# A graph network and a mixture of experts on one core: the experts' second layer as three products of halves, split on chip

## What is computed

```python
# x: (16, 512, 128), adj: (16, 512, 512), all float32
x = x + gnn(layernorm(x), adj)      # convolution of 17 taps, exp(-dist) * adj, GRU gates
x = x + ffn(layernorm(x))           # 8 experts, top 2 of them per token
# in ffn, with xn normalized once more, gamma and beta applied, w_full the weights of the two chosen experts:
for e in range(8):
    h = gelu(xn @ W1[e] + b1[e], approximate=False)      # 128 -> 256
    y = y + (h @ W2[e] + b2[e]) * w_full[..., e, None]   # 256 -> 128
```

## Time and profile before

| | us |
|---|---|
| median of the runs | 666.71 |
| lowest and highest | 663.08, 667.06 |
| the profiled execution, its own time | 669.05 |
| its span on the core | 667.3 |

### The profile page before, as it was taken

How to read it: one execution, slowest core, us unless ns; L and a number is a source line. 1 busy time by engine, 2 the same in 40 slices (tenths; PEclk the granted TensorE clock), 3 DMA queues, 4 the chain that set the end, 5 groups by cost and what they waited for, 6 DMA issues and landing times.

```text
span 667.3 us, 13068 instructions
## 1 busy us (share of the span) xinstructions
PE 623.3 (93%) x3784; PEld 530.2 (79%) x3784; DVE 498.2 (75%) x2050; ACT 418.4 (63%) x824; POOL 344.6 (52%) x273
## 2 busy tenths in 40 slices
PE   3799898989999999999999999999999988799996
PEld 2679687777979797979797888888888777688874
DVE  6958888888888888888888888888888755333322
ACT  4544546485858485858485858585767546466663
POOL 3200314145847474748474747574757545556750
PEclk9898999999999999999999999999999979899999
DMA  8327231538379747474755666666555578863341
GB/s 305 115 92 245 82 124 52 179 101 232 75 203 340 195 117 189 122 191 120 182 130 152 154 153 159 156 156 158 149 140 153 147 184 200 224 144 53 52 77 57
DMA packets 105399, 101.04 MB, mean 151 GB/s; under 512 B 8896, under 2 KB 83904, under 8 KB 105024
## 3 DMA queue, kind: packets, MB, share of 16 engines
q1 hardware_dynamic: 82736, 83.28, 40.4%
q0 software_dynamic: 22592, 16.92, 16.7%
HBM read 75.85 MB, written 30.51 MB: 159 GB/s over the span
## 4 chain that ended last, share of the span: by engine, by line
PE 63%; DVE 17%; issue 7%; DMA 5%; POOL 4%; ACT 3%; SPq 0%; another core or an unknown queue 0%; DVEq 0%; ACTq 0%; POOLq 0%
PE Y L598 9%; PE G L708 5%; PE C L530 5%; PE C L531 5%; PE C L532 5%; PE G L530 4%; PE G L532 4%; PE G L531 4%; PE G L598 4%; POOL routed L1013 2%; DMA x_ln<-x 2%; DMA out<-y_t,xt 2%; PE H L573 2%; PE Y L606 2%; PE H L574 2%
## 5 line engine op out<-in xcount | busy, mean ns | idle before, releaser
L978 POOL DMA_INDIRECT out<-y_t,xt x96 | 157.5, 1641 | 130.7 <-DMA out<-y_t,xt 85.9
L1013 POOL DMA_INDIRECT routed<-row,at_u x112 | 118.6, 1059 | 119.8 <-DVE at_u L1207 86.9
L530 PE MATMUL C<-cv_h,w_hi 128*128 128x256 f32 (+1 forms) x432 | 131.2, 304 | 2.2 <-DVE cv_l L1068 1.3
L531 PE MATMUL C<-cv_l,w_hi 128*128 128x256 f32 (+1 forms) x432 | 124.5, 288 | 0.0
L532 PE MATMUL C<-cv_h,w_lo 128*128 128x256 f32 (+1 forms) x432 | 124.3, 288 | 0.0
L530 PEld LDWEIGHTS C<-cv_h,w_hi 128*128 128x128 f32 x432 | 82.7, 191 | 4.8 <-issue 2.2
L531 PEld LDWEIGHTS C<-cv_l,w_hi 128*128 128x128 f32 x432 | 82.7, 191 | 1.3
L532 PEld LDWEIGHTS C<-cv_h,w_lo 128*128 128x128 f32 x432 | 82.7, 191 | 0.7
L598 PE MATMUL Y<-ge,w_t 128*128 128x256 f32 x228 | 62.0, 395 | 6.0 <-DVE y_t L1307 3.5
L708 PE MATMUL G<-ex,msg_t 128*128 128x512 f32 x128 | 58.9, 603 | 0.3 <-ACT gh L901 0.3
L598 PEld LDWEIGHTS Y<-ge,w_t 128*128 128x128 f32 x228 | 39.4, 192 | 24.0 <-issue 20.5
(11 more groups left out here) (264 smaller groups left out, 1692.8 us busy)
## 6 DMA issues: line engine op xcount, KB each, us to landing
w_t<-w_all SPq DMA_DIRECT2D x66, 256.0 KB
adj<-adj_t SPq DMA_DIRECT2D x16, 1024.0 KB
xt<-routed SPq DMA_DIRECT2D x66, 144.0 KB
w_t<-w_all SPq DMA_DIRECT2D x66, 136.0 KB
x_ln<-x SPq DMA_DIRECT2D x16, 256.0 KB, 6.3
x_res<-x SPq DMA_DIRECT2D x16, 256.0 KB
out<-x SPq DMA_DIRECT2D x15, 256.0 KB
wd<-w_all SPq DMA_DIRECT2D x10, 256.0 KB
```

The lines of the kernel that those rows point to most:

```text
L530: pe.matmul(psum, hi(w), rhs_h, start=start, stop=False)
L531: pe.matmul(psum, hi(w), rhs_l, start=False, stop=False)
L978: nc.gpsimd.indirect_dma_start(out=out, out_offset=bass.IndirectOffsetOnAxis(ap=xt[j][:, t, R_ID:R_ID + 1].bitcast(U32), axis=0), in_=y_t[ ...
L1013: nc.gpsimd.indirect_dma_start(out=routed, out_offset=bass.IndirectOffsetOnAxis(ap=at_u[:, n:n + 1], axis=0), in_=row[:, n // TOP, :], in_ ...
```

## The change

The second layer is done as the first: `ge` is split into `ge_h` (rounded to fp32r) and `ge_l` (the rest), the weights W2 likewise, and for each half of the hidden units there are three products. `second` waits for `ge_split` in place of `gelu_done`. The high half is rounded by ScalarE right behind gelu (`hidden_hi`), for the dense items of one kind only (the last graph's second half); for the others VectorE rounds (`dense_hidden_split`). VectorE always makes the low half (`hidden_lo`).

The expert's weights, both layers' halves, biases and one-hot row, are one block of 1040 columns (520 KB) with one DMA, where two DMAs brought 784 columns (392 KB); W2's halves are made in graph 1 (ScalarE) and graph 2 (VectorE), and the store moves from the head of graph 1 to graph 2 (SP's order). There are three buffers for dense weights in place of two, and four more `pick_w` and `own_w`. SP loads `x_ln` before `adj`. In TensorE's order `tile_b(1)` stands behind `conv_diff(14, 17)`. In the last part the first layer runs two items ahead of the second layer, where it ran one ahead, and the turn three.

VectorE's order changes: `tile_hidden(0)` is first in the iteration, `tile_hidden(1)` behind the normalizing, the statistics of the graph after the next stand behind the batch norm and ahead of xlT_l, the weighing of tile 1 ahead of xc_l, the choice is in two parts with `tile_hidden(2)` between, and the weighing of tile 2 is ahead of the gate's sum, `tile_hidden(3)` behind it.

```diff
+            def second(m, w):
+                pe.wait_ge(ge_split, m + 1)
                 if m > 0:
                     pe.wait_ge(y_done, m if m <= STREAMED else m - 1)
+                y = YO[bank_set(m)][:, 0:TILE]
                 for h in range(HALVES):
-                    last = pe.matmul(YO[bank_set(m)][:, 0:TILE], w2[:, h * P:(h + 1) * P], ge[m % 2][:, h, :],
-                                     start=(h == 0), stop=(h == HALVES - 1))
+                    w_hs, w_ls = (w[:, first + h * P:first + (h + 1) * P] for first in (X_W2, X_W2_LO))
+                    pe.matmul(y, w_hs, ge_h[m % 2][:, h, :], start=(h == 0), stop=False)
+                    pe.matmul(y, w_hs, ge_l[m % 2][:, h, :], start=False, stop=False)
+                    last = pe.matmul(y, w_ls, ge_h[m % 2][:, h, :], start=False, stop=(h == HALVES - 1))
                 last.then_inc(pe_y, 1)
...
-                conv_diff(4, 14)
+                conv_diff(4, TAPS)
                 tile_b(1)
-                conv_diff(14, TAPS)
...
-            for i in range(-2, len(items) + 1):
+            for i in range(-3, len(items) + 1):
...
                     else:
-                        dense_hidden(*items[i + 1])
+                        dense_hidden(*items[i + 2])
...
+            def hidden_hi(m):
+                act.wait_ge(gelu_done, m + 1)
+                if m >= 2:
+                    act.wait_ge(pe_y, m - 1)
+                nc.scalar.copy(ge_h[m % 2][:], ge[m % 2][:]).then_inc(ge_hi, 1)
...
+            def hidden_lo(m, hi_done, count):
+
+                dve.wait_ge(hi_done, count)
+                nc.vector.tensor_tensor(ge_l[m % 2][:], ge[m % 2][:], ge_h[m % 2][:].bitcast(F32),
+                                        ALU.subtract).then_inc(ge_split, 1)
+
+            def dense_hidden_split(m):
+                dve.wait_ge(gelu_done, m + 1)
+                dve.wait_ge(pe_y, m - 1)
+                nc.vector.tensor_copy(ge_h[m % 2][:], ge[m % 2][:]).then_inc(ge_dense_hi, 1)
+                hidden_lo(m, ge_dense_hi, on_vector[m])
...
                 if more:
                     normalize_x(g + 1)
+                tile_hidden(1)
...
+                if more and not is_graph(g, GRAPHS - 2):
+                    statistics_x(g + 2)
+                expert_weights()
                 if more:
                     split_lo(g + 1)
+                tile_weigh(1)
...
-            for k in range(2):
+            for k in range(DENSE_BUFFERS):
                 dense_loads(k)
```

More of the change, by code:

```diff
@@ L381, in gnn_moe, with rounded_on_scalar @@
         items = list(last_items())
+        def rounded_on_scalar(item):
+            return len(item) == 4 or (item[1] == DENSE - 1 and item[3] == 1)
+        on_scalar = {item[0]: STREAMED + i + 1 for i, item in enumerate(filter(rounded_on_scalar, items))}
+        on_vector = {m: i + 1 for i, m in enumerate(item[0] for item in items if item[0] not in on_scalar)}
         number = {item[1]: item[0] for item in items if len(item) == 4}
@@ L1391, in tile_weigh @@
                         weigh(n)
+                tile_hidden(0)
                 tile_split(1)
@@ L1526, in _ @@
             d = GRAPHS - 1
[L1527 removed]
+            choose, take_two, place = router_steps(d)
             sums = {}
             dve.wait_ge(pe_nmp, GRAPHS)
[L1530 to L1532 removed]
+            for i in range(-3, len(items) + 1):
+                if i + 3 < len(items) and is_tile(items[i + 3]):
+                    m, n, j, loads = items[i + 3]
                     tile_lo(n, bank_set(m))
```

229 lines of the change are left out of this document (122 added, 107 removed).

## The result

| | us |
|---|---|
| kernel before, median (lowest, highest) of the runs beside it | 665.88 (663.08, 667.06) |
| changed kernel, median (lowest, highest) | 676.18 (674.55, 685.32) |
| ratio, with its 95% interval | 1.015 (1.0128 to 1.0172) |

The account below looks back on a forecast made before the run. The prediction took TensorE's instructions as the bound in streamed graphs and last part. Streamed graphs +7, last part -12 and graphs 0 to 3 -2 made -7 us from the median of 666.71: 659.7 us, range 647 to 674.

Parts of the forecast that it names:

- Streamed graphs, +7: Eleven streamed graphs, each +0.7 us: 1.0 wait at tile 1, 0.1 smaller waits, 0.1 lateness, less 0.5 saved on TensorE.
- 13.72: Streamed graph: us from VectorE's weighing of tile 3 to the end of tile 1's low half, making TensorE wait 1.0.
- The first rival: No wait at tile 1, as waits between VectorE's small steps give way: 648 us, chance 0.17.
- the third rival: VectorE bounds the streamed graphs: 2.5 us wait at tile 1, +2.1 us a graph, 676 us, chance 0.18.
- now all of such lateness is paid: Streamed graphs: lateness from VectorE's varying small steps reaches TensorE in full, counted as 0.1 us on average per graph.
- The last part, -12: Tiles and dense items after the streamed graphs: pace -7, load stall -6, roots wait -1, start +2; between -18 and -3.
- The steady pace: Last part: cheaper second layer saves 0.18 us per item over 38 items, -7 us; dense items every 1.97 us.
- the second rival: Last part gains only its stall, as ScalarE or VectorE's fuller order keeps the pace at 2.1: 668 us, chance 0.2.
- The stall of 4.43 us at a dense load: Last part: TensorE's wait for the third dense load goes with three buffers, and the slow clock after it: -6 us.
- my +2: Start of the last part: first tile's second layer waits for the fourth's turn, VectorE fuller; between 0 and 5 us.
- Graphs 0 to 3, -2: Earlier statistics remove waits for cv_l, gaining up to 2.7 us; weight splitting takes some back; between -3 and +2.
- the ring at the end: Last dense items, 2.18 us each: second layer 0.93, turned back 0.38, weighing 0.61, 0.15 to the next second layer.

Follow-up runs that it names:

- e6: Changed kernel with weight loads of 392 KB in place of 520, the second layer's low-half weights zero: 1.0178 of the kernel before.
- e11: Kernel before with weight loads of 520 KB in place of 392, the added columns unused: 1.0053 of the kernel before.
- e13: Kernel before with a tile's expert weights, the same 392 KB, in one DMA in place of two: 1.0096 of the unedited kernel.
- e14: Changed kernel with each 520 KB weight block in two DMAs in place of one: 1.0168 of the kernel before.
- e9: Change in the last part only, split ahead of the tile's low half; streamed graphs in full float32, old orders, one-DMA loads of 392 KB: 1.0168 of the kernel before.
- e16: e9 with two DMAs per weight block in place of one: 1.0016 of the kernel before.
- e12: Changed kernel with the second of two padding-row stores issued two graphs later: 1.0137 of the kernel before, 674.97 us.
- e1: Changed kernel again, nothing edited, on another chip: 1.0168 of the kernel before.
- e2: Changed kernel; in the last part VectorE splits an item's hidden values ahead of the low half of the tile three items on: 1.0184 of the kernel before.
- e3: Changed kernel with ScalarE rounding the hidden values of every item of the last part: 1.026 of the kernel before.
- e18: e15 with the last graph's normalized rows written one item later on ScalarE: 0.9905 of the kernel before, 659.1 us.
- e5: Kernel before, unedited, profiled on another chip: one run, 667.7 us.
- e7: Changed kernel; in streamed graphs VectorE makes the low half for one of 256 tokens only, the rest zero: 1.0099 of the kernel before.
- e8: e2's edit, plus tile 1's low half ahead of tile 0's weighing and the next graph's normalization in streamed graphs: 1.0203 of the kernel before.
- e17: e16 with the last graph's normalized rows written one item later on ScalarE: 0.9984 of the kernel before.
- e4: Changed kernel with all eight scatters of rows to the experts ahead of tile 2's add on GpSimd: 1.069 of the kernel before.
- e15: e14 with e2's order in the last part: 1.0045 of the kernel before.

## Why the prediction was wrong

**The step that failed.** "The loads carry 520 in place of 392 KB per tile, but two DMAs in place of three per tile, and run ahead by some ten us; I count nothing, and 4 us if that lead is gone." That is said of the last part; for the streamed graphs the sum has no term for the DMAs at all. In place of nothing stood about 11 us in one graph, and not by the bytes (e6, e11): with one DMA fewer per tile SyncE's issues come 2 us earlier against GpSimd's add, the next add waits for the one before, and scatters, normalized rows and TensorE follow. That the number of DMAs does it is shown by e13 (this one edit: stall, 1.0% slower) and e14 (the reverse: no stall), and by e9 and e16, 1.0168 and 1.0016 with only the second DMA between them, though on two chips. In e14 itself the time is not better than the changed kernel's; its period is 34.8, with the wait at tile 1.

That it is the padding stores is an observation and not an experiment. Of the 20 profiles 12 have 2.2 us or more between the add and the first store and no wait of the next add, 8 have 0.7 or less and 4.4 to 6.9 us of it; but the tile loads go out just ahead of these stores in every run and shift with them, and no run moves both stores alone (e12 moved the second, and the stall stayed). For the stores speaks that without them, in the 18 profiles other than the changed kernel's and e6's, no add that was waited for took over 9.2 us to the next, tile loads beside it or not; with them all eight took 11.6 to 14.1. The kernel before already had 0.98 us of ScalarE's wait for the rows, at 217.77, so there was no slack; I had looked for waits on TensorE's path and passed over a small one at the end of a chain of DMAs.

The second stall of the profiled execution, at 540 us, has no padding store beside it. Far ahead of it one add's own instruction on GpSimd took 4.23 us in place of 1.56, and the next two adds each waited 6 us:

```profile
496.99 4.23 POOL L998 DMA_INDIRECT out<-y_t,xt  x1 [0.31 <-issue]
507.35 1.55 POOL L998 DMA_INDIRECT out<-y_t,xt  x1 [6.14 <-DMA out<-y_t,xt]
```

In e6's profile the stall near 416 us also comes behind such an instruction, of 4.64 us at 371.79. What makes them long is open, and e12 has no such stall.

**How the sum came out.** With e12's profile against the one before, from graph 4's `x_res` load to the loop's last tile it is +7.3 where I had +7, but by luck: 10.9 of it are the stall, and the rest of that stretch is 3.6 shorter. The last part with its tail is -2.2 (-3.3 in the changed kernel's own profile) where I had -12, and the graphs ahead +0.6 where I had -2. So a second term is mis-sized by as much as the stall, the last part's; it is taken up below.

**Streamed graphs, +7 (1.0 us of wait at tile 1, -0.5 of TensorE).** In the changed kernel's profile neither is there. VectorE from the weighing of tile 3, TensorE at tile 1, in the changed kernel:

```profile
316.40 0.42 DVE L1341 TENSOR_TENSOR y_t<-Y,own_w 128x256 f32<-128x256 f32 x1 [0.47 <-PE Y L614]
...
328.80 0.68 DVE L1314 TENSOR_TENSOR ge_l<-ge,ge_h 128x512 fp32r<-128x512 f32 x1
329.40 2.48 DVE L1461 TENSOR_TENSOR ex<-ex,adj 128x512 f32<-128x512 f32 x4
```

```profile
329.53 0.39 PE L605 MATMUL Y<-ge_h,w_t 128*128 128x256 f32 x1
329.76 0.28 PE L606 MATMUL Y<-ge_l,w_t 128*128 128x256 f32 x1
...
330.35 0.60 PE L546 MATMUL G<-cst,row 128*128 128x128 f32 x4
```

The low half ends 13.08 us after the weighing, where I had 13.72, and TensorE starts 0.05 us after that, some 0.2 later than its last convolution product would let it: it hardly waits, but it has no slack either. What I had too much is a gap. I had read the stretch of 11.98 us of the kernel before as one with "hardly a gap", and it has this one:

```profile
283.17 0.17 DVE L1115 SCALAR_TENSOR_TENSOR rs<-rt_t,rs 128x8 f32<-128x8 f32 x1 [0.49 <-DVE rt_t L1112]
```

That step starts 0.92 us behind the step whose result it needs (L1112, 282.25); in the changed kernel's graph it is 0.26, and the 0.66 between the two is about the 0.64 by which my 13.72 was too long. The first rival, that the waits between the small steps give way, was right in this for that profile. The price of `ge_l` was right, 0.60 from start to start, with 0.68 of duration. (The Trainium skill's page "VectorE: DVE Perf Modes", section "The DRAIN you can't avoid", says that the next operation does not start until the pipeline is empty, but also that one that is not held starts earlier. The prediction left out the second half; these rows fit it.) The six products take 0.82 to the next start at tile 1 and not 0.72, since the first takes 0.23; that is 0.05 less than the 0.87 of before. Tile 0 has 0.79 in place of 0.87, and tile 2, behind the float32 product with the adjacency, 1.12 where before had 0.75 and 0.19 more in the product behind it. So TensorE gains nothing in all, and the period is that of before.

In the profiles of e1, e2, e3 and e14 the gaps in VectorE's small steps are there, and the wait is 1.2 to 2.1 us in most graphs. That is above my 1.0, and the periods of 34.7 to 35.4 against 33.5 make it +1.2 to +1.9 a graph, under the third rival's +2.1. The mechanism ("now all of such lateness is paid") was right. Its average of 0.1 us was right in the changed kernel's profile, e12 and e18, and ten times too small on the chips of e1 and e14. The kernel before, e5, e7, e8, e13 and e16 have such gaps too. Each chip was used for one batch of runs, so chip and time can't be told apart, and what sets the gaps is open.

**The last part, -12: measured -3.3 with its tail.** The steady pace was to fall by 0.18 for 38 items, -7; it rose by 0.09 for 22 mixed items, +2, and fell by 0.15 for the dense ones behind them, -2, so this term gave nothing. The rise is the second rival's mechanism, VectorE's fuller order in the place of TensorE. I had said of these items that "VectorE is fuller" and still counted the 0.18: the time for the split is there on VectorE, but the order put it ahead of a weighing that TensorE waits for. e2 shows it: with the split moved ahead of the tile's steps the pace is 1.99. The dense items at the end were to come every 1.97:

```profile
663.20 0.36 PE L605 MATMUL Y<-ge_h,wd 128*128 128x256 f32 x1 [0.15 <-DVE x L1354]
...
665.23 0.36 PE L605 MATMUL G<-ge_h,wd 128*128 128x256 f32 x1
```

They take 2.03, with a second layer of 0.79 in place of the 0.72. The stall of 4.43 us at a dense load is gone, as forecast. The wait for the roots, forecast to shrink by 1, grew from 2.25 to 3.27: with one more item of lead ScalarE writes the rows ahead of the rounding of a later tile, and e17's edit takes 1 us off it. It also has the granted clock at 0.58 behind it (580 to 584 us), where a second layer took 1.42 us. From the loop's last second layer to the first of the last part it is 7.5 us where it was 6.6, within my +2.

**Graphs 0 to 3, -2.** Graph 4's `x_res` is at 153.34 and was at 152.63: nothing gained. The three waits for `cv_l` (1.00, 0.95 and 0.77 us) are gone, as forecast. In their place TensorE stands 1.16 us for `pre` in graph 2, and the first tile of all waits 2.15 us for its low half, at 140.81, where its second layer stood 0.78 before.

**The rivals.** None was it. The third gave the measured time, 676, which is luck: its wait of 2.5 us at tile 1 is not in that profile. The second was right in its mechanism for the mixed items, the first in that the gap at tile 1 gave way.

**Slips in the working.** The four parts of the ring at the end add up to 2.07 and not 2.18, since from turning back to weighing it is 0.49 from start to start and not 0.38. The first rival's terms give 647 and not 648. By the third rival's own terms the kernel gets slower than before from a wait of 1.7 us and not 1.8. The chances put 0.29 of the forecast's 0.45 on the faster side, which is not "about halves". None of this changes what is said above.

## What to carry to other kernels

When an edit removes or merges DMA issues, lay the queues of all issuing engines side by side and look at what large transfer now falls beside a chain of small dependent DMAs; a wait of one microsecond at the end of such a chain means that there is no slack. A new operation on an engine that shares a ring with TensorE belongs ahead of the steps that wait for a third engine, not behind them: here that was 0.18 us in each item. With VectorE at 92% and no slack at tile 1, gaps between its small steps went on into TensorE's waits, and the profiles of some chips had such gaps and those of others had none: measure on more than one before believing 1%.

## What was unexpected of the hardware

- With the padding stores issued beside an add of 256 rows by indirect DMA (0.7 us behind its second half or ahead of it), the next add could go only 11.6 to 14.1 us after that half. With them issued 2.2 us or more behind it, the next add found it landed when GpSimd's own queue came to it, 7.1 to 8.2 us after the half in eight of twelve profiles and 10.1 to 16.4 in e2, e3, e4 and e7. The Trainium skill's page "DMA: Bandwidth & Descriptors", section "Queues, rings and completion order", says that each DMA engine goes round robin between its queues, packet by packet. From that alone I would not expect 2 us more or less in SyncE's issue to matter so much; why it does, no run here shows.
- The same loop had a period of 33.5 us in e12 and e18 and of 34.7 to 35.2 in e1, e14 and e15, with the long operations of VectorE as before (`ge_l` 683 to 687 ns, the multiplications with the adjacency 675 to 680 ns); the difference is gaps of 0.2 to 1.1 us between the small dependent steps.
- The first of the six fp32r products took 0.19 to 0.23 us to the next start where TensorE had stood before it, and at tile 0 of a graph also without that; in the last part, where it came right behind the product before, it took 0.12 like the others (as at 584.93 us), and the six took 0.68 to 0.72 in place of 0.76 to 0.82.
